# Expert stages of a six-stage block: VectorE makes both halves of the 0/1 routing matrix

## The chip, the cores and the metric

One core of one Trainium2 chip. The time is the device time of one execution of the whole kernel in microseconds. Five engines run their own instruction streams and meet at semaphores: PE (TensorE, with its weight loads shown apart as PEld), DVE (VectorE), ACT (ScalarE), POOL (GpSimd) and SP (SyncE, which here issues DMAs).

## The reference

The input x is 32 batches of 256 tokens with 128 channels. Six sub-layers follow one another: half a feed-forward layer, a gated attention unit, half a feed-forward layer, half an expert layer, linear attention, and half an expert layer again. Only the two expert layers bear on this case:

```
logits = x @ router_w + router_b                      # 8 experts
top_k_logits, expert_indices = top_k(logits, 2)
expert_probs = softmax(top_k_logits)
one_hot = one_hot(all first choices, then all second choices of a batch)
pos = cumsum(one_hot) * one_hot - 1                    # place of each token at its expert
expert_inputs[expert, pos] += x                        # 76 places for each expert and batch
o = (silu((in @ w_fc + b_fc) * (in @ w_gate + b_gate))) @ w_proj + b_proj
y = sum over the two choices of prob * o[expert, pos]
x = x + 0.5 * y
```

A place past the 76th is dropped. 8 experts of 76 places make 608 places ("slots") for each batch.

## The kernel before

A batch is two tiles (t = 0, 1) of 128 tokens, one token to a partition. An expert stage (`moe_stage`, run twice, as stages moe3 and moe5) groups the 32 batches into eight chunks of 2, 3, 5, 5, 5, 5, 5 and 2 batches. For one chunk, the eight experts are worked through one after another ("units"), each with four steps of the hidden dimension, so a chunk is 32 steps, here called work slots, numbered 0 to 31. In each work slot PE makes two products with 76 columns for each batch of the chunk (380 columns for five): `up`, L1538 and L1542. ACT adds a bias to the first (L1611), DVE multiplies both into `act` (L1715, `multiply`), ACT applies silu (L1618). At the end of each unit (every fourth work slot) PE makes the second layer of the unit before (`down`, L1552), DVE adds its bias (L1724) and SP stores the rows to memory.

Between these steps, the next chunk's batches are routed and the last chunk's results are brought back. The order is written out beforehand: each engine goes through the same list of work slots and does its own part of what is listed there. For the batch with index i of the next chunk the list says, counted from work slot 5i (9i in the first chunk and the one before the last): norm at +0, transpose at +1, router at +2, mask at +3, count at +4, assign at +5, hot0 at +8, hot1 at +9, send0 at +10, send1 at +11. In chunks with a step of 5, the hot0 of a batch and the mask of the next one share a work slot. Within a work slot DVE does first `multiply`, then norm, router, mask, assign, hot, `combine`, and then the bias of `down`; PE does first `up`, then router, transpose, count, send, and then `down`.

The parts that the change touches:

- `assign` (DVE) computes for each token the numbers of its two slots: `slot[..., 0:1]` for the first choice, `slot[..., 1:2]` for the second, and signals `routed` (L1697).
- `first_choice` (POOL, L1447) compares the row of slot numbers 1 to 608 with the first slot of each token and writes 0 or 1 in bf16 to `hot`, one instruction of 128x608 for each tile. POOL does it in its own order right after the `split` of the batch that has its norm in the same work slot, since it has nothing to do in hot0 and hot1: it is listed under assign (+5).
- `second_choice` (DVE, L1705) waits for `hot_first` (POOL's tile is there) and adds the comparison with the second slot to the same tile, at hot0 for tile 0 and at hot1 for tile 1.
- `send` (PE, L1526) waits for both tiles of `hot` and multiplies the tokens, split by POOL into three bf16 parts (`split`, L1436 to L1439), with `hot`: six matmuls for each half of the slots. ACT copies the result to `rowsT` (L1602), from which the next chunk's `up` reads.
- `hot` has two buffers. The one that writes first to a buffer waits for `sent_ps`, that the batch two before has been sent.
- `gather` (POOL, L1456): four indirect DMAs for each batch bring expert results back; `combine` (DVE, L1733) adds them to x. POOL gets to a gather five work slots ahead of its combine.

At the start of a stage, before the first work slot, the two batches of chunk 0 are routed with nothing beside them; `up` can't begin until both have been sent.

## Time and profile before

| | |
|---|---|
| Median of 3 runs | 2491.58 us (2489.34 to 2493.92) |
| Profiled execution, its own time | 2514.78 us |
| Its span, first to last instruction | 2512.8 us, 47937 instructions |
| Expert stages in that span | about 514 to 1070 us and 1916 to 2512 us |
| Mean granted TensorE clock | 0.967 of full speed |

The profiled execution took 23.2 us (0.9%) more than the median of the runs. All durations below are from the profiled execution. "Busy" is the time in which an engine had an instruction in work. A row of the timeline gives the start in us from the start of the span, the time in us, the engine, the source line, the operation, what it writes and what it reads, how many instructions were merged into the row, and in brackets the idle time of the engine just before and what ended it. "issue" there means that the profile shows nothing that the engine waited for.

### The profile page before, as it was taken

The numbers are of one execution on the slowest core, as the hardware profiler recorded it, in microseconds if no ns is written. First come the engines' busy times: TensorE is split into PE (matmuls) and PEld (weight loads), VectorE is DVE, ScalarE is ACT, GpSimd is POOL, SyncE is SP. The second block draws the span as 40 slices with busy tenths as digits, with TensorE's granted clock in tenths as the row PEclk, the third lists the DMA queues.
The fourth block names the chain that finished last, engine by engine and source line by source line (L and its number), as shares of the span: only waits on it lengthen the run. The fifth ranks groups of instructions, "written<-read, shape, count | busy, mean of one in ns | idle before, by whom it ended". The sixth has DMA issues, their size and how long they took to land.

```text
span 2512.8 us, 47937 instructions
## 1 busy us (share of the span) xinstructions
PE 2272.8 (90%) x14854; PEld 1816.3 (72%) x14854; DVE 1588.7 (63%) x4974; ACT 1312.6 (52%) x2713; POOL 733.7 (29%) x818
## 2 busy tenths in 40 slices
PE   3979998968999999849999999999996889999994
PEld 3979997957767676637777777777775776776773
DVE  5867776766667775435655656565655666767653
ACT  3755556744444444326666666666662544444441
POOL 2202220045546765320000000000002455766543
PEclk9989999989999999879999999999998999999997
DMA  7040000000111111100000000000000001111122
GB/s 242 0 159 0 0 0 0 0 5 23 26 28 40 41 36 41 46 18 1 0 0 0 0 0 0 0 0 0 0 0 0 15 25 35 43 50 45 49 56 50
DMA packets 70867, 67.45 MB, mean 27 GB/s; under 512 B 9696, under 2 KB 58336, under 8 KB 70368
## 3 DMA queue, kind: packets, MB, share of 16 engines
q1 hardware_dynamic: 61504, 47.16, 5.9%
q0 software_dynamic: 8192, 16.79, 2.9%
q10 hardware_dynamic: 1056, 2.10, 0.3%
q8 instruction: 56, 0.92, 0.2%
q14 instruction: 59, 0.48, 0.1%
HBM read 31.94 MB, written 34.08 MB: 26 GB/s over the span
## 4 chain that ended last, share of the span: by engine, by line
PE 48%; issue 4%; DVE 2%; POOL 1%; ACT 1%; DMA 0%; another core or an unknown queue 0%; ACTq 0%; POOLq 0%; DVEq 0%
PE moe_bank L1552 5%; PE lin_bank L983 5%; PE moe_bank L1538 5%; PE lin_bank L903 5%; PE moe_bank L1542 5%; PE lin_bank L911 4%; PE lin_bank L930 4%; PE lin_bank L922 4%; PE lin_bank L959 3%; PE lin_bank L975 2%; PE moe_bank L1526 2%; PE lin_bank L946 1%; POOL moe_landed L1456 1%; ACT lin_xT L1049 0%; PE moe_bank L1493 0%
## 5 line engine op out<-in xcount | busy, mean ns | idle before, releaser
L1611 ACT ACTIVATE moe_fc<-moe_bank,all_b_fc 128x380 f32<-128x380 f32 (+2 forms) x512 | 262.3, 513 | 341.7 <-PE moe_bank L1538 286.8
L1715 DVE SCALAR_TENSOR_TENSOR moe_act<-moe_bank,all_b_moe_gate,moe_fc 128x380 f32<-128x380 f32 (+2 forms) x512 | 271.0, 531 | 221.4 <-PE moe_bank L1542 106.9
L1538 PE MATMUL moe_bank<-moe_rowsT,all_w_fc 128*128 128x380 f32 (+2 forms) x1024 | 357.3, 431 | 15.6 <-ACT moe_fc L1611 12.8
L1542 PE MATMUL moe_bank<-moe_rowsT,all_w_gate 128*128 128x380 f32 (+2 forms) x1024 | 351.7, 425 | 12.9 <-DVE moe_act L1715 7.7
L1552 PEld LDWEIGHTS moe_bank<-all_w_proj,moe_act 128*128 128x128 f32 x2688 | 321.6, 195 | 12.4 <-ACT moe_act L1618 1.8
L1552 PE MATMUL moe_bank<-all_w_proj,moe_act 128*128 128x128 f32 x2688 | 329.2, 279 | 1.4 <-ACT moe_act L1618 1.4
L1456 POOL DMA_INDIRECT moe_landed<-rows_out,moe_take_at x256 | 266.0, 1039 | 176.2 <-issue 174.6
L1542 PEld LDWEIGHTS moe_bank<-moe_rowsT,all_w_gate 128*128 128x128 f32 x1024 | 188.3, 193 | 101.6 <-DVE moe_act L1715 8.9
L1447 POOL TENSOR_SCALAR moe_hot<-all_slot_ids,moe_slot 128x608 bf16<-128x608 f32 x128 | 233.3, 1830 | 91.7 <-issue 54.9
L1618 ACT ACTIVATE moe_act<-moe_act 128x760 f32<-128x760 f32 (+2 forms) x256 | 181.5, 709 | 96.0 <-DVE moe_act L1715 88.8
L1148 POOL COPY lin_xn_ones<-lin_xn 128x254 f32<-128x254 f32 x32 | 12.7, 398 | 748.0 <-PE lin_bank L911 743.3
L1053 ACT ACTIVATE lin_neg<-lin_bank 128x512 f32<-128x512 f32 x256 | 151.7, 592 | 95.3 <-PE lin_bank L903 50.7
L1538 PEld LDWEIGHTS moe_bank<-moe_rowsT,all_w_fc 128*128 128x128 f32 x1024 | 167.9, 193 | 43.6 <-ACT moe_fc L1611 13.5
L959 PEld LDWEIGHTS lin_bank<-lin_kv,lin_qT 128*128 128x128 f32 x1024 | 144.4, 191 | 63.4 <-issue 54.1
L1057 ACT ACTIVATE lin_neg<-lin_neg 128x512 f32<-128x512 f32 x256 | 161.1, 630 | 7.9
L1526 PE MATMUL moe_bank<-moe_hot,moe_parts 128*128 128x304 bf16 x768 | 125.5, 301 | 40.4 <-issue 24.7
L1081 ACT ACTIVATE lin_gate_tanh<-lin_bank,all_bg_half 128x256 f32<-128x256 f32 x256 | 103.5, 468 | 108.3 <-PE lin_bank L930 108.2
L1724 DVE TENSOR_TENSOR moe_expert_out<-moe_bank,all_b_proj 128x384 f32<-128x384 f32 (+1 forms) x128 | 64.8, 506 | 142.9 <-PE moe_bank L1552 108.4
L959 PE MATMUL lin_bank<-lin_kv,lin_qT 128*128 128x130 f32 x1024 | 151.9, 275 | 1.1 <-DVE lin_heads L1196 0.8
L1526 PEld LDWEIGHTS moe_bank<-moe_hot,moe_parts 128*128 128x128 bf16 x768 | 72.5, 100 | 96.3 <-issue 69.1
L903 PE MATMUL lin_bank<-all_wk,lin_xT 128*128 128x512 f32 x256 | 128.9, 607 | 4.5 <-ACT lin_xT L1049 2.7
L451 ACT ACTIVATE ffn_hT<-ffn_bank,all_b,all_alpha 128x256 f32<-128x256 f32 x256 | 123.6, 564 | 17.2 <-PE ffn_bank L407 17.2
(222 smaller groups left out, 4309.2 us busy)
## 6 DMA issues: line engine op xcount, KB each, us to landing
rows_out<-moe_expert_out SPq DMA_DIRECT2D x80, 128.0 KB
rows_out<-all_zeros SPq DMA_DIRECT2D x1, 9728.0 KB, 28.0
rows_out<-moe_expert_out SPq DMA_DIRECT2D x80, 62.0 KB
moe_landed<-rows_out,moe_take_at POOLq DMA_INDIRECT x256
out<-all_x SPq DMA_DIRECT2D x5, 640.0 KB
rows_out<-moe_expert_out SPq DMA_DIRECT2D x48, 64.0 KB
all_w_fc<-in_w_fc SPq DMA_DIRECT2D x1, 2048.0 KB, 9.8
all_w_gate<-in_w_gate SPq DMA_DIRECT2D x1, 2048.0 KB, 13.7
```

The costliest lines, as they stand in the source:

```text
L903: nc.tensor.matmul(bank[j][:, :], xT[:, j // 2 * P:(j // 2 + 1) * P], k.wk[:, j % 2 * HU:(j % 2 + 1) * HU], start=True, stop=True).then_in ...
L959: last = nc.tensor.matmul(bank[4 + n % 2][:, i * 2 * DH1:(i + 1) * 2 * DH1], qT[:, p, t * P:(t + 1) * P], kv[:, p, :], start=True, stop=True)
L1057: nc.scalar.activation(neg[:, j, :], neg[:, j, :], ACT.Exp, scale=-1.0).then_inc(exps.sem, 1)
L1447: nc.gpsimd.tensor_scalar(hot[:, b % 2, t, :], k.slot_ids[:, :], slot[:, b % 2, t, 0:1], None, ALU.is_equal).then_inc(hot_first, 1)
L1456: nc.gpsimd.indirect_dma_start(landed[:, b % LANDED, t, h, :], None, k.rows_out, bass.IndirectOffsetOnAxis(take_at[:, i, h:h + 1], 0), bou ...
L1526: last = nc.tensor.matmul(bank[SENT][:, 0:HALF], parts[:, b % PARTS, q, t, :], hot[:, b % 2, t, h * HALF:(h + 1) * HALF], start=(t == 0 an ...
L1538: nc.tensor.matmul(bank[FC + j % 2][:, 0:c.width], k.w_fc[:, e, j * P:(j + 1) * P], rowsT[:, c.n % 2, e, 0:c.width], start=True, stop=True ...
L1542: nc.tensor.matmul(bank[GATE + j % 2][:, 0:c.width], k.w_gate[:, e, j * P:(j + 1) * P], rowsT[:, c.n % 2, e, 0:c.width], start=True, stop= ...
L1552: last = nc.tensor.matmul(bank[OUT][:, j * DIM:(j + 1) * DIM], act_in[:, i % 2, h, j * P:(j + 1) * P], k.w_proj[:, e * MC + h, :], start=( ...
L1611: nc.scalar.activation(fc[:, j, 0:c.width], bank[FC + j % 2][:, 0:c.width], ACT.Identity, bias=k.b_fc[:, e * MC + j:e * MC + j + 1]).then_ ...
L1618: nc.scalar.activation(a, a, ACT.Silu).then_inc(act_sb, 1)
L1715: nc.vector.scalar_tensor_tensor(act_in[:, i % 2, j, 0:c.width], bank[GATE + j % 2][:, 0:c.width], k.b_moe_gate[:, e * MC + j:e * MC + j + ...
```

## The change

VectorE makes both comparisons. `first_choice` and its semaphore are gone from POOL's program. In DVE's hot0 and hot1, and in its start of the stage, `second_choice` becomes `choices`: it compares with the first slot, waits for that result, and then adds the comparison with the second one. The wait for the buffer of the batch two before moves from POOL to DVE. `choose_masks` no longer waits for POOL's comparisons of the batch two before. `assign`, `send` and all work slots stay as they are.

```
             @block.gpsimd
-                def first_choice(b):
-                    pool.wait_ge(routed, b + 1)
-                    if b >= 2:
-                        pool.wait_ge(sent_ps, 2 * (b - 2) + 2)
-                    for t in range(TILES):
-                        nc.gpsimd.tensor_scalar(hot[:, b % 2, t, :], k.slot_ids[:, :], slot[:, b % 2, t, 0:1], None,
-                                                ALU.is_equal).then_inc(hot_first, 1)
...
-                for b in plan[0].batches:
-                    first_choice(b)
...
-                        if "assign" in work:
-                            first_choice(work["assign"])
...
             @block.vector
                     if b >= 2:
-                        dve.wait_ge(hot_first, TILES * (b - 1))
                         dve.wait_ge(count_ps, b - 1)
...
-                def second_choice(b, t):
-                    dve.wait_ge(hot_first, TILES * b + t + 1)
+                def choices(b, t):
                     dve.wait_ge(routed, b + 1)
+                    if b >= 2:
+                        dve.wait_ge(sent_ps, 2 * (b - 2) + 2)
+                    link(nc.vector.tensor_scalar(hot[:, b % 2, t, :], k.slot_ids[:, :], slot[:, b % 2, t, 0:1], None, ALU.is_equal))
                     nc.vector.scalar_tensor_tensor(hot[:, b % 2, t, :], k.slot_ids[:, :], slot[:, b % 2, t, 1:2], hot[:, b % 2, t, :],
                                                    ALU.is_equal, ALU.add).then_inc(hot_sb, 1)
...
                     for t in range(TILES):
-                        second_choice(b, t)
+                        choices(b, t)
...
                             if f"hot{t}" in work:
-                                second_choice(work[f"hot{t}"], t)
+                                choices(work[f"hot{t}"], t)
```

`link` gives the instruction a semaphore and lets DVE wait for it before its next instruction.

## Rows read from the trace of the kernel before

**Rows 1.** The page, part 1: busy time of each engine and share of the span.

```profile
PE 2272.8 (90%) x14854; PEld 1816.3 (72%) x14854; DVE 1588.7 (63%) x4974; ACT 1312.6 (52%) x2713; POOL 733.7 (29%) x818
```

**Rows 2.** Windows, one chunk: PE, PEld, DVE, ACT, POOL busy; clock; DMA share; GB/s.

```profile
740.00:817.00 77.00, 75.64 (x446) 54.40 (x445) 55.55 (x185) 36.41 (x68) 50.57 (x50) 1.00 0.15 39
```

**Rows 3.** Groups of instructions: busy us, mean ns | idle before, releasers.

```profile
L1447 POOL TENSOR_SCALAR moe_hot<-all_slot_ids,moe_slot 128x608 bf16<-128x608 f32 x128 | 233.3, 1830 | 91.7 <-issue 54.9 <-DVE moe_slot L1697 32.8
...
L1526 PE MATMUL moe_bank<-moe_hot,moe_parts 128*128 128x304 bf16 x768 | 125.5, 301 | 40.4 <-issue 24.7 <-DVE moe_hot L1705 12.0 <-ACT moe_rowsT L1602 3.2
...
L1705 DVE SCALAR_TENSOR_TENSOR moe_hot<-all_slot_ids,moe_slot,moe_hot 128x608 bf16<-128x608 f32 x128 | 112.9, 882 | 4.6 <-POOL moe_hot L1447 3.9 <-issue 0.2
...
L1436 POOL CAST moe_parts<-moe_xn 128x256 bf16<-128x256 f32 x64 | 28.1, 439 | 247.8 <-DVE moe_xn L261 176.2 <-issue 71.2
```

**Rows 4.** Timeline of the second expert stage: a send (chunk of five, first batch).

```profile
2152.62 0.61 DVE L1715 SCALAR_TENSOR_TENSOR moe_act<-moe_bank,all_b_moe_gate,moe_fc 128x380 f32<-128x380 f32 x1 [0.82 <-PE moe_bank L1542]
...
2153.60 0.85 DVE L1705 SCALAR_TENSOR_TENSOR moe_hot<-all_slot_ids,moe_slot,moe_hot 128x608 bf16<-128x608 f32 x1
...
2154.36 0.61 DVE L1715 SCALAR_TENSOR_TENSOR moe_act<-moe_bank,all_b_moe_gate,moe_fc 128x380 f32<-128x380 f32 x1
2154.58 0.80 PE L1542 MATMUL moe_bank<-moe_rowsT,all_w_gate 128*128 128x380 f32 x2
...
2154.88 0.84 DVE L1705 SCALAR_TENSOR_TENSOR moe_hot<-all_slot_ids,moe_slot,moe_hot 128x608 bf16<-128x608 f32 x1
...
2155.80 0.64 PEld L1526 LDWEIGHTS moe_bank<-moe_hot,moe_parts 128*128 128x128 bf16 x6 [1.03 <-issue]
2155.83 0.93 PE L1526 MATMUL moe_bank<-moe_hot,moe_parts 128*128 128x304 bf16 x6 [0.45 <-issue]
```

**Rows 5.** Timeline: the same of the chunk's third batch.

```profile
2179.29 0.84 DVE L1705 SCALAR_TENSOR_TENSOR moe_hot<-all_slot_ids,moe_slot,moe_hot 128x608 bf16<-128x608 f32 x1
...
2181.98 0.10 PEld L1526 LDWEIGHTS moe_bank<-moe_hot,moe_parts 128*128 128x128 bf16 x1
```

**Rows 6.** Timeline: the same of the chunk's fourth batch.

```profile
2192.60 0.61 DVE L1715 SCALAR_TENSOR_TENSOR moe_act<-moe_bank,all_b_moe_gate,moe_fc 128x380 f32<-128x380 f32 x1 [0.82 <-PE moe_bank L1542]
```

**Rows 7.** Groups of DVE instructions, shapes kept apart.

```profile
L261 DVE TENSOR_SCALAR ffn_xn<-all_x,ffn_mean,ffn_rstd 128x128 f32 x128 | 38.7, 345 | 13.8 <-issue 11.8
...
L773 DVE TENSOR_SCALAR gau_lin_qT<-gau_qkT,all_os_gamma,all_os_beta 128x256 f32<-128x256 f32 x33 | 13.6, 411 | 0.0
...
L384 DVE CAST all_tri<-all_tri_in 128x128 bf16<-128x128 f32 x1 | 0.2, 228 | 0.0
```

**Rows 8.** Timeline: two instructions of `assign` joined by `link`.

```profile
2157.12 0.17 DVE L1694 TENSOR_SCALAR moe_over<-moe_pos 128x4 f32<-128x4 f32 x1
2157.32 0.36 DVE L1695 SCALAR_TENSOR_TENSOR moe_over<-moe_top_atf,moe_over 128x4 f32<-128x4 f32 x1
```

**Rows 9.** Timeline: DVE beside POOL's comparisons, splits and gathers.

```profile
702.61 3.60 POOL L1447 TENSOR_SCALAR moe_hot<-all_slot_ids,moe_slot 128x608 bf16<-128x608 f32 x2
...
705.56 0.68 DVE L1679 CAST moe_top_atf<-moe_top_at 128x4 f32<-128x4 uint32 x1
...
2155.62 1.00 POOL L1456 DMA_INDIRECT moe_landed<-rows_out,moe_take_at  x1 [0.30 <-issue]
...
2156.16 0.60 DVE L261 TENSOR_SCALAR moe_xn<-all_x,moe_mean,moe_rstd 128x128 f32<-128x128 f32 x2
```

**Rows 10.** Timeline: start of the first expert stage.

```profile
529.06 0.68 DVE L1699 TENSOR_SCALAR moe_prob<-moe_tanh_gap 128x2 f32<-128x2 f32 x1
...
531.54 1.35 DVE L1705 SCALAR_TENSOR_TENSOR moe_hot<-all_slot_ids,moe_slot,moe_hot 128x608 bf16<-128x608 f32 x1 [0.43 <-POOL moe_hot L1447]
...
533.04 1.68 PE L1526 MATMUL moe_bank<-moe_hot,moe_parts 128*128 128x304 bf16 x6 [6.01 <-DVE moe_hot L1705]
```

**Rows 11.** Timeline: second batch routed beside the chunk of three (228 columns).

```profile
609.92 0.15 DVE L1684 SCALAR_TENSOR_TENSOR moe_row_base<-moe_top_atf,all_batch_row 128x4 f32<-128x4 f32 x1
610.78 1.35 DVE L1705 SCALAR_TENSOR_TENSOR moe_hot<-all_slot_ids,moe_slot,moe_hot 128x608 bf16<-128x608 f32 x1 [0.70 <-POOL moe_hot L1447]
```

More of the change, by code:

```diff
@@ L1341, in moe_stage @@
         routed = k.sem("routed")
-        hot_first = k.sem("first_choice_hot")
         hot_sb = k.sem("hot_ready")
```

## The prediction

> **What bounds the kernel now.** I began with the page's busy times: PE has 90% of the span [rows 1]. An average over six stages doesn't decide, so the next view was the windows, one for each chunk of an expert stage. In a chunk of five batches PE is busy 75.64 of 77 us at full clock, DVE 55.55, POOL 50.57 [rows 2]. There, whatever holds PE lengthens the kernel, and little else does. The third view was the groups: PE's send (L1526) has 40.4 us of idle time before it, 24.7 of it "issue", and 12.0 put down to DVE's hot. DVE waits for POOL's comparisons only 3.9 us in all [rows 3].
>
> "issue" names no culprit, so the last view was the timeline around each of the 64 sends. There the second comparison of tile 1 starts at 2154.88 and takes 0.84 [rows 4], so it ends at about 2155.73 (to the ns of the trace). The send's first weight load starts at 2155.80, 0.07 us later, and PE had been idle 0.45 us. I read the same pair for all batches: in 50 of 64 the weights come 0.07 us after the end of hot1. The send waits for hot in nearly every batch; the profile just doesn't say so. The DVE chain in front is pinned to PE at its head: the multiply of hot0's work slot begins after 0.82 us of idle time, upon PE's product [rows 4]. From there DVE works without a gap (multiply, masks, hot0, multiply, hot1) until hot1 is done, and PE can't start the send. Anything put into this chain goes into the time of PE, and PE has no idle time elsewhere in the chunk to take it back: 77 less 75.64 us, most of it these very waits.
>
> **What the change removes.** POOL loses 128 comparisons of 1.83 us, 233.3 us of busy time [rows 3]. POOL is no bound in the chunks [rows 2]: they are done before DVE needs them, but for 8 waits of 3.9 us together, and they start right behind the split. Worth nothing by themselves. They hinder DVE, though: see below.
>
> **What it adds.** 128 comparisons on DVE, one operand in SBUF in f32, one pointer scalar, 608 elements, bf16 out. The trace has no such instruction, so I size it from relatives [rows 7]. The same kind with two pointer scalars takes 345 ns for 128 elements and 411 for 256: 66 ns for 128 elements, 0.515 ns each. To 608 elements that is 345 + 480 x 0.515 = 592 ns with two pointers. A cast to bf16 without pointers takes 228 ns for 128 elements, so each pointer costs about 58 ns, and one pointer gives 592 - 58 = 0.53 us. Bounds: without any pointer's cost 0.475, with both 0.59; and if a comparison ran at the pace of L1705, 0.844 [rows 4], a far upper bound, since L1705 reads two tensors. I take 0.53, from the rows of the same kind. `link` then makes the second comparison wait: an instruction of 0.17 from 2157.12 is followed by its reader at 2157.32, 0.03 us after its end [rows 8]. Each tile adds d = 0.53 + 0.035 = 0.565 us. The added waits (routed, the send of two batches before) are long fulfilled: the send in question is at work slot 5i+1, hot0 at 5i+8.
>
> What queues behind it: on DVE the multiply of the next work slot. PE needs that one only for the product two work slots on, after the send, so it holds nothing before the send does. Behind the send wait all later products of PE, in order. They move by the same amount as DVE's chain, both from the end of hot1, so no second stall is to be expected.
>
> **The sum, batch by batch**, over the 60 batches that are routed inside work slots:
> - 8 batches have their hot1 early: 2179.29 + 0.84 = 2180.13 against a send at 2181.98 [rows 5]. PE is in `down` and has 1.85 us (1.57 in one) of other work. Two tiles cost 1.13: nothing.
> - 7 batches are like [rows 6]: between hot0 and hot1 DVE waits 0.82 us for PE's product behind a `down`. The tile of hot0 disappears in that; one counts: 7d.
> - 2 batches have 0.735 us to spare (2d - 0.735 each), 1 has 0.43 (2d - 0.43), 2 have 0.14 (2d - 0.14 each).
> - 2 batches are like [rows 11], where hot0 waited for POOL. The comparison could begin at 610.00, hot1 would be done at 610.00 + 2d + 1.98 instead of 612.56 + 0.85 = 613.41: 2d - 1.43 each.
> - The other 40 pay both tiles: 80d.
>
> Together 97d - 5.0 = 54.8 - 5.0 = 49.8 us.
>
> **The start of each stage.** The first send came at 533.04 after 6 us of waiting for hot, DVE waited for POOL's tiles 0.43 at a time, and its comparison took 1.35 instead of 0.84 beside POOL's [rows 10]. Now DVE is free for the first tile at about 529.2 (the 0.68 of L1699 is such a hindrance too), and two tiles of 1.41, overlapped by 0.08, end at 531.94 instead of 532.89. Gain 0.9 for each stage, 1.8 in all; the second batch's send is held by PE and ACT.
>
> **DVE beside POOL.** A DVE cast of four elements took 0.68 us instead of 0.16 until POOL's comparison ended (702.61 + 3.60 = 706.21) [rows 9]. It lies in the chain of one of the 40 batches, once in each stage: 1.0 us gained. The other such delays (combine has most of them) end in DVE idle time before the next multiply. Against it, in the stretches with a step of nine, norm stands just before hot1; POOL's split (0.44 for its first piece, L1436 [rows 3]) gets between first and second comparison in 6 batches, 0.4 each: 2.4 us lost.
>
> Sum: 49.8 - 1.8 - 1.0 + 2.4 = +49.4 us. The profiled execution should go from 2514.8 to about 2564, the median, 23 us lower and on the same program, from 2491.6 to 2541.0 (+2.0%).
>
> **The gathers.** Before, a gather started after POOL's comparisons and ran beside hot0 and hot1; now it starts about 3.6 us earlier, right after the split, and combine's data land earlier. Combine isn't in the chain, so no gain. Whether a gather holds up the new comparison must be asked: in rows 9 two instructions of that kind took 0.60 for both, their usual pace, in the midst of a gather's instruction; of 43 such meetings the median is 342 ns, as without one. So I add nothing.
>
> The Trainium skill, page "SBUF — State Buffer", section "Who interferes with whom", says that a VectorE instruction in a mode with two ports and any GpSimd instruction shut each other out for the whole instruction. The cast that waited for POOL's comparison agrees; the two instructions beside the gather don't, if the gather's instruction counts. Applied to gathers too, the rule makes the second rival below.
>
> **Rivals.**
> 1. *The comparison runs at the pace of L1705*: 0.844 us, d = 0.88. Then 97 x 0.88 - 5.0 = 80.4, the start gains only 0.3 for each stage: 80.4 - 0.6 - 1.0 + 2.4 = +81, 2573 us. Against it speaks the slope of 0.515 ns in rows 7, for it that no comparison stands among these rows. Chance 0.08.
> 2. *Gathers hold up the comparison.* A gather's instruction takes 1.00 [rows 9]; half of it on average for each of the 97 tiles in the chain would be +49 more: 2590 us. The 43 meetings speak against it. Chance 0.04.
> 3. *Part is given back.* If ACT or the second send had a wait that the delay now fills, half might return: +25, 2516 us. For it: PE idles in other places as well, around `count`. Against it: 1.4 us in 77 is all there is [rows 2]. Chance 0.10.
> 4. *The other side: no slower.* The 0.07 us could be what the send's own start costs, with PE held by its queue ("issue" in rows 4), and not by hot1. Then the 0.45 us before the send cover part of 1.13, the spare time the rest, and only the start's 1.8 and the 1.0 are left: 2489 us, which is within what this kernel's measurement can tell from no change (0.2%, 5 us). It would take over from the forecast if fewer than 5 / 0.565 = 9 tiles lay in the chain. Against it: 50 equal distances of 0.07 with idle times of PE between 0.04 and 2.2. Chance 0.06, of which 0.02 for a gain over 0.2%.
> 5. *Something beyond, such as DVE becoming the bound.* 55.55 + 10 x 0.53 = 61 of then 81 us in a chunk: no [rows 2]. Chance 0.02, slower.
>
> **How the numbers follow.** The forecast has 0.70 and from the bounds of d (0.51 to 0.625, so 97d - 5.0 from 44 to 56) its own range of 2535 to 2548. Cases 1 and 3 enclose it at 2573 and 2516; with them the range 2516 to 2574 leaves out about 0.12 and the edges of those two. Slower by over 0.2%: 0.70 + 0.08 + 0.04 + 0.10 + 0.02 = 0.94; within 0.2% 0.04; faster 0.02.
>
> **What would show it.** The new comparison 128x608 at about 0.53 us, the one behind it 0.03 later at 0.84. The send's weights still 0.07 after hot1 and PE idle about 1.6 before it where rows 4 have 0.45; the third batch of each chunk unchanged. A chunk of five takes 77 + 7 x 0.565 = 81 us, with 75.6 of PE busy as before. POOL's busy time falls by 233 us, to 500. The prediction is wrong if the comparison is far from 0.53, if the chunk doesn't grow by 4 us, or if the idle time before the send grows but shrinks elsewhere.

## The result and the profile after

| | before | after |
|---|---|---|
| Median | 2492.75 us (2489.34 to 2494.98, 4 runs) | 2544.11 us (2541.59 to 2544.87, 4 runs) |
| Ratio | | 1.0206, 95% interval 1.0194 to 1.0219 |
| Profiled execution, its own time | 2514.78 us | 2544.87 us |

The change costs 51.4 us; the prediction said 49.4 (2541.0, range 2516 to 2574). The two profiled executions are only 30 us apart, and the profiled one of after is 19 us below the 2564 that the prediction gave for it: the one of before lost some 22 us, over both expert stages, in waits put down to "remote" behind the last send of a stage, and the one of after has none of these. The sections below therefore compare distances between sends, which lie ahead of those waits. Of all executions reported here one, of experiment 3, is far off the others (7893 us against 2489 to 2499), and nothing on record explains it.

The page's first part and one chunk as a window (the counterparts of [rows 1] and [rows 2]; the window is now 81 us wide, columns as there):

```profile
PE 2275.4 (89%) x14854; PEld 1817.8 (71%) x14854; DVE 1638.8 (64%) x5102; ACT 1313.8 (52%) x2713; POOL 500.8 (20%) x690
```

```profile
740.00:821.00 81.00, 75.58 (x446) 54.28 (x445) 59.38 (x196) 36.61 (x68) 31.87 (x40) 1.00 0.14 35
```

POOL has lost 232.9 us of busy time and 128 instructions. The same chunk, with the same 446 matmuls and the same busy time of PE at full clock, takes 81 us instead of 77. PE does no more; it waits more.

The groups of the comparisons with their shapes kept apart, and then the page's group of the send (the counterparts of [rows 3]):

```profile
L1692 DVE TENSOR_SCALAR moe_hot<-all_slot_ids,moe_slot 128x608 bf16<-128x608 f32 x128 | 68.1, 532 | 0.1
L1693 DVE SCALAR_TENSOR_TENSOR moe_hot<-all_slot_ids,moe_slot,moe_hot 128x608 bf16<-128x608 f32 x128 | 109.0, 852 | 4.6
```

```profile
L1513 PE MATMUL moe_bank<-moe_hot,moe_parts 128*128 128x304 bf16 x768 | 129.3, 308 | 84.2 <-issue 71.0
```

The new comparison takes 532 ns on average (forecast 0.53). The idle time ahead of the send has doubled, 40.4 to 84.2 us, and nearly all of the increase has no culprit in the profile: "issue" went from 24.7 to 71.0. The timeline names it. This is the send of [rows 4], 26 us later by now:

```profile
2177.37 0.61 DVE L1703 SCALAR_TENSOR_TENSOR moe_act<-moe_bank,all_b_moe_gate,moe_fc 128x380 f32<-128x380 f32 x1 [0.82 <-PE moe_bank L1529]
...
2178.30 0.99 POOL L1447 DMA_INDIRECT moe_landed<-rows_out,moe_take_at  x1 [0.30 <-issue]
2178.42 0.53 DVE L1692 TENSOR_SCALAR moe_hot<-all_slot_ids,moe_slot 128x608 bf16<-128x608 f32 x1
2178.98 0.85 DVE L1693 SCALAR_TENSOR_TENSOR moe_hot<-all_slot_ids,moe_slot,moe_hot 128x608 bf16<-128x608 f32 x1
2179.74 0.61 DVE L1703 SCALAR_TENSOR_TENSOR moe_act<-moe_bank,all_b_moe_gate,moe_fc 128x380 f32<-128x380 f32 x1
2180.27 0.53 DVE L1692 TENSOR_SCALAR moe_hot<-all_slot_ids,moe_slot 128x608 bf16<-128x608 f32 x1
2180.83 0.85 DVE L1693 SCALAR_TENSOR_TENSOR moe_hot<-all_slot_ids,moe_slot,moe_hot 128x608 bf16<-128x608 f32 x1
2181.75 0.64 PEld L1513 LDWEIGHTS moe_bank<-moe_hot,moe_parts 128*128 128x128 bf16 x6 [2.23 <-issue]
2181.78 0.94 PE L1513 MATMUL moe_bank<-moe_hot,moe_parts 128*128 128x304 bf16 x6 [1.66 <-issue]
```

The chain still begins with 0.82 us of waiting for PE and has no gap. The last comparison ends at 2181.68, the send's weights come 0.07 us later, and PE's idle time went from 0.45 to 1.66 us. The third batch of the chunk (the counterpart of [rows 5]) still has time to spare:

```profile
2207.51 0.85 DVE L1693 SCALAR_TENSOR_TENSOR moe_hot<-all_slot_ids,moe_slot,moe_hot 128x608 bf16<-128x608 f32 x1
...
2209.07 0.10 PEld L1513 LDWEIGHTS moe_bank<-moe_hot,moe_parts 128*128 128x128 bf16 x1
```

Its comparison ends at 2208.36, 0.71 us ahead of the send, where 1.85 us were spare before: the difference is 1.14, two tiles. I took the distance from each send to the next in both traces (start of the first weight load):

| stretch | before, us | after, us | difference |
|---|---|---|---|
| to a full batch (for example the 17th) | 12.20 | 13.34 | +1.14 |
| to a third batch | 13.98 | 13.98 | 0.00 |
| to a fourth batch | 12.06 | 12.63 | +0.57 |
| to the batch with index 13, either stage | 12.48 | 13.10 | +0.62 |
| 40 steady distances (ends at index 10 to 29, both stages) | 617.6 | 651.4 | +33.8 |
| 18 distances in the chunks of 2 and 3 (ends at index 1 to 9) | 227.1 | 239.8 | +12.7 |
| last two of each stage | 95.3 | 100.3 | +5.0 |
| all 62 | 940.0 | 991.4 | +51.4 |

The start of the first stage, up to its first send (the counterpart of [rows 10]):

```profile
528.42 0.54 DVE L1692 TENSOR_SCALAR moe_hot<-all_slot_ids,moe_slot 128x608 bf16<-128x608 f32 x1
...
530.33 0.85 DVE L1693 SCALAR_TENSOR_TENSOR moe_hot<-all_slot_ids,moe_slot,moe_hot 128x608 bf16<-128x608 f32 x1
...
531.33 1.68 PE L1513 MATMUL moe_bank<-moe_hot,moe_parts 128*128 128x304 bf16 x6 [5.02 <-DVE moe_hot L1693]
```

The send comes 1.71 us earlier, but the stage itself began 0.73 us earlier in this execution, as POOL's first instruction of the stage shows (before, after):

```profile
514.40 2.66 POOL L1465 MEMSET moe_act<- 128x3072 f32 x1 [123.77 <-POOLq L319]
```

```profile
513.67 2.66 POOL L1456 MEMSET moe_act<- 128x3072 f32 x1 [123.77 <-POOLq L319]
```

Counted from there, the first send is 0.99 us earlier in the first stage and 0.97 in the second.

**One thing that the prediction had no term for** is the clock. The windows from 541 to 590 us, before and after:

```profile
541.00:590.00 49.00, 42.28 (x334) 38.05 (x333) 29.36 (x117) 25.23 (x67) 20.27 (x22) 1.00 0.04 12
```

```profile
541.00:590.00 49.00, 40.78 (x307) 36.95 (x307) 28.66 (x110) 22.05 (x59) 6.63 (x11) 0.93 0.04 11
```

PE gets through 307 matmuls instead of 334, and the mean granted clock is 0.93 instead of 1.00. The timeline shows a stretch; first the 16 weight loads of a `down` after, then the same `down` before:

```profile
568.27 1.00 PE L1513 MATMUL moe_bank<-moe_hot,moe_parts 128*128 128x304 bf16 x6 [0.95 <-issue]
...
568.91 3.48 PEld L1539 LDWEIGHTS moe_bank<-all_w_proj,moe_act 128*128 128x128 f32 x16
```

```profile
568.01 1.88 PEld L1552 LDWEIGHTS moe_bank<-all_w_proj,moe_act 128*128 128x128 f32 x16
```

3.48 instead of 1.88 us: the clock is at the lower level, 1.2 GHz. Ahead of it PE had been idle for 0.95 us before the send and for 1.54 shortly before that. From the first product of each stage to 30 us before its last, the clock stands at the lower level for 6.8 us before (two places) and 30.7 us after (nine). What one such place costs can be read from the trace of after, since both stages run the same program: the distance to the batch with index 7 is 12.34 us in the first stage, with 3.4 us at the lower level in it, and 10.64 in the second, with none; the one to index 10 is 26.86 with none and 28.53 with 3.4 us. So a place costs about 1.7 us, half of its length, and the seven more places about 12 us. Of these seven, four lie in the chunks of 2 and 3, one in a steady distance, and one right behind the last send of each stage.

### The profile page after: what moved, and what is told of

Its sections match the earlier page's. It is cut to its first block, busy times and chain, and to the rows that moved or that the text cites. A ratio compares the mean times of both kernels' runs of the same rounds, so it can differ in the third digit from the quotient of the medians.

```text
span 2542.8 us, 47839 instructions
## 1 busy us (share of the span) xinstructions
PE 2275.4 (89%) x14854; PEld 1817.8 (71%) x14854; DVE 1638.8 (64%) x5102; ACT 1313.8 (52%) x2713; POOL 500.8 (20%) x690
## 4 chain that ended last, share of the span: by engine, by line
PE 46%; issue 5%; DVE 2%; ACT 1%; POOL 1%; DMA 0%; ACTq 0%; POOLq 0%; DVEq 0%
PE moe_bank L1539 5%; PE lin_bank L983 5%; PE lin_bank L903 5%; PE lin_bank L911 4%; PE lin_bank L930 4%; PE moe_bank L1525 4%; PE lin_bank L922 4%; PE moe_bank L1529 4%; PE lin_bank L959 3%; PE lin_bank L975 2%; PE moe_bank L1513 2%; PE lin_bank L946 1%; POOL moe_landed L1447 1%; ACT lin_xT L1049 0%; PE moe_bank L1480 0%
## 5 line engine op out<-in xcount | busy, mean ns | idle before, releaser
L1529 PE MATMUL moe_bank<-moe_rowsT,all_w_gate 128*128 128x380 f32 (+2 forms) x1024 | 351.5, 425 | 10.9 <-DVE moe_act L1703 10.9
L1539 PEld LDWEIGHTS moe_bank<-all_w_proj,moe_act 128*128 128x128 f32 x2688 | 323.4, 196 | 12.5 <-ACT moe_act L1605 1.6
L1529 PEld LDWEIGHTS moe_bank<-moe_rowsT,all_w_gate 128*128 128x128 f32 x1024 | 188.1, 192 | 99.7 <-DVE moe_act L1703 14.1
L1513 PE MATMUL moe_bank<-moe_hot,moe_parts 128*128 128x304 bf16 x768 | 129.3, 308 | 84.2 <-issue 71.0
L1513 PEld LDWEIGHTS moe_bank<-moe_hot,moe_parts 128*128 128x128 bf16 x768 | 73.5, 102 | 142.1 <-issue 113.9
L1589 ACT COPY moe_rowsT<-moe_bank 128x304 f32<-128x304 f32 x128 | 52.8, 413 | 185.9 <-PE moe_bank L1513 185.9
L1435 POOL CAST moe_parts<-moe_xn 128x256 bf16<-128x256 f32 x64 | 26.7, 418 | 565.5 <-DVE moe_xn L261 360.7
```

Source lines behind the costliest of these rows:

```text
L1513: last = nc.tensor.matmul(bank[SENT][:, 0:HALF], parts[:, b % PARTS, q, t, :], hot[:, b % 2, t, h * HALF:(h + 1) * HALF], start=(t == 0 an ...
L1529: nc.tensor.matmul(bank[GATE + j % 2][:, 0:c.width], k.w_gate[:, e, j * P:(j + 1) * P], rowsT[:, c.n % 2, e, 0:c.width], start=True, stop= ...
L1539: last = nc.tensor.matmul(bank[OUT][:, j * DIM:(j + 1) * DIM], act_in[:, i % 2, h, j * P:(j + 1) * P], k.w_proj[:, e * MC + h, :], start=( ...
```

## The experiments

Nine kernels in twelve runs, three groups of four, each group on one chip with the kernel before beside it: 2494.72 us in the first group, 2520.13 in the second, 2515.64 in the third (13 executions each). On the first chip no trace has waits put down to "remote" in the expert stages; on the other two all have (experiment 7), so a time of the first group can't be compared with one of the others, only distances without such a wait can.

**1. The first comparison twice** (first group), the changed kernel with

```
-                    link(nc.vector.tensor_scalar(hot[...], k.slot_ids[:, :], slot[..., 0:1], None, ALU.is_equal))
+                    for _ in range(2):
+                        link(nc.vector.tensor_scalar(hot[...], k.slot_ids[:, :], slot[..., 0:1], None, ALU.is_equal))
```

> The comparison with the first slot is made twice for each tile (the output stays the same). Theory 1 (everything put between the multiply of hot0's work slot and the end of hot1 goes into PE's time): a second d of 0.57 us for each of the 97 tiles that lie in the chain, 55 us, and since the spare time of the 8 'third' batches (0.70 us left in the changed kernel) and of the 7 'fourth' ones (0.25 left) is now exceeded, 8 x 0.43 + 7 x 0.32 = 5.7 more: +61 over the changed kernel, 2605 us, the weights of the send still 0.07 us after hot1. Rival (the slowdown of the change is not DVE's chain but something that came once, such as another layout of the instruction streams or PE's clock): less than +20, below 2565.

Measured: 2639.62 us, ratio 1.0575 (1.0556 to 1.0594), +95 us over the changed kernel. In the undisturbed steady batches the second comparison costs what the first did or less: 12.26 to 13.40 us, 13.34 to 14.49, the fourth 12.63 to 12.92, and now the third too, 13.98 to 14.49, since its spare time is used up. For the rest, the time at the lower clock rose from 31 to 99 us, now in the steady chunks as well. There 12 of the 40 distances hold 3.1 to 5.8 us of it; these are 1.5 to 2.8 us longer than the same distance without it (15.97 instead of 14.49, 16.12 instead of 14.49), 20 us together, and no other distance is. At half of its length, as in the trace of after, (99 - 31) / 2 = 34 us is the gap between +95 and the +61 of the theory. The waits of PE, of this kernel:

```profile
PE moe_bank L1513 <- issue: 126.0, 52, 3.6
```

So the work in the chain is paid in full, and the lower clock comes on top. That PE's longer idling brings it is the candidate that experiment 5 asks about.

**2. DVE makes the first comparison of tile 0 only**, POOL that of tile 1 (first group), the kernel before with

```
-                    for t in range(TILES):
+                    for t in range(1, TILES):
                         nc.gpsimd.tensor_scalar(hot[:, b % 2, t, :], ...).then_inc(hot_first, 1)
...
+                    if t:
+                        dve.wait_ge(hot_first, b + 1)
+                    else:
+                        link(nc.vector.tensor_scalar(hot[:, b % 2, t, :], ..., ALU.is_equal))
```

> The kernel before, but VectorE makes the first comparison of tile 0 (at hot0) and GpSimd that of tile 1. Theory 1: tile 0's comparison counts in the 40 full batches and in 3 others, not in the fourth batches of the chunks of five, where DVE waits 0.82 us for PE between hot0 and hot1: 43 x 0.565 - 0.7 = +24, 2516 us. Rival (what costs is that DVE has any such instruction beside gathers, or the sum of its work): the same per tile everywhere, 60 of 120 tiles, half of the measured +51, with the fourth batches paying as well.

Measured: 2512.32 us, ratio 1.0070 (1.0054 to 1.0087). The full batches grow by 0.58 (12.20 to 12.78), the fourth ones not at all (12.06 both), the third ones neither. In the steady chunks that is the prediction's count tile by tile: tile 0's comparison disappears in DVE's wait of 0.82 us between hot0 and hot1 in the fourth batches, and is paid in the full ones. The sum was missed, +17.6 us instead of +24: the chunks of 2 and 3 grew by 0.7 us, where the count has 13 tiles less 0.7, 6.6 us. The lower clock doesn't explain it: it took 19.7 us of these 18 distances, and 21.5 in the kernel before.

**3. The first comparisons where DVE has time** (first group): both still on DVE, but at work slots +5 and +6 of the batch, the second ones left at +8 and +9.

```
-"hot0": 8, "hot1": 9,
+"first0": 5, "first1": 6, "hot0": 8, "hot1": 9,
...
+                            if f"first{t}" in work:
+                                first(work[f"first{t}"], t)
                             if f"hot{t}" in work:
-                                choices(work[f"hot{t}"], t)
+                                second(work[f"hot{t}"], t)
```

> The changed kernel with the same 128 comparisons on VectorE, but moved ahead in its list: tile 0 at +5 behind assign, tile 1 at +6; the second comparisons stay at hot0 and hot1. Theory 1: DVE has idle time there before hot0's work slot, so the chain from multiply to hot1 is as long as before the change, and the whole +51 is gone: 2490 us, 3 below before through the start of the stages and the missing hindrance by GpSimd. Rival 1 (VectorE has too much work, wherever it stands): 2544 as in the changed kernel. Rival 2 (half of the idle time is too short for it): about 2505.

Measured: 2494.22 us, ratio 0.9996 (0.9986 to 1.0006). The same 128 comparisons on the same engine cost nothing, although they are slower there, 622 ns on average instead of 532; the distances between sends are those of the kernel before. PE's wait is back as well:

```profile
PE moe_bank L1513 <- issue: 22.9, 48, 1.2
```

This is the strongest run for the theory: not the work of DVE costs, but its place behind a product of PE and in front of a send. VectorE having too much to do (rival 1) is out. It was run on the first group's chip alone.

**4. Both comparisons of both tiles earlier**, at +6 and +7 (first group).

```
-"hot0": 8, "hot1": 9,
+"hot0": 6, "hot1": 7,
```

> The changed kernel with hot0 at +6 and hot1 at +7 in place of +8 and +9, send unchanged at +10 and +11. Theory 1: the send finds hot ready, its weights come right behind the product before, and PE's idle time before the sends, 24 us over both stages in the kernel before, is gone as well: 2466 us, faster than both. Rival 1 (the 0.07 us is the send's own start, the idle time stays): 2490 at best. Rival 2 (hot0 beside combine makes the multiplies late, and PE waits for these instead): 2490 to 2540, with PE's idle time before the products of L1529.

Measured: 2515.41 us, ratio 1.0074 (1.0054 to 1.0094). The theory's 2466 is missed by 49 us, and the time lies in the range of rival 2. The wait before the send is gone ("issue" no longer stands among the waits of L1513), but another has come, and not at the products of L1529, where the rival had it:

```profile
PE moe_bank L1497 <- DVE moe_mask L1666: 51.1, 45, 2.5
```

PE's `count` stands one work slot after DVE's mask; at +7 of a batch the next batch has its router, at +8 its mask, and the hot instructions in front make the mask late. The send's wait was moved to `count`. A step of this list is free only if nothing behind it in DVE's order feeds PE soon.

**5. Two comparisons, with PE kept at work** (second group, and again in the third): the kernel of 1, with six more matmuls into the send's bank before PE waits for hot; their result is overwritten. The wait for that bank (`sent_sb`) had to move ahead of the one for hot with them, and the third batches of the chunks of five have no such matmuls.

```
+                    if b or h:
+                        pe.wait_ge(sent_sb, 2 * b + h)
...
+                        for q in range(6):
+                            nc.tensor.matmul(bank[SENT][:, 0:HALF], parts[...], parts[...], start=True, stop=True)
                         pe.wait_ge(hot_sb, TILES * (b + 1))
-                    if b or h:
-                        pe.wait_ge(sent_sb, 2 * b + h)
```

> As the kernel with the comparison made twice (2640 us, 34 more than the waits alone should give), but PE fills part of each long wait before a send with six matmuls of 304 columns whose result is overwritten (0.94 us at full clock; left out in the third batches of the chunks of five, where there is no such wait). Theory 1a (the 34 us are half-clock stretches that follow PE's waits: 96 us at 0.5 in that kernel between the sends, 31 in the changed kernel, 7 before): with shorter idle times the half-clock stretches shrink to under 30 us, the sends stay where DVE puts them, and the time falls by about 30 us to 2608. Rival (DVE's chain itself got longer than it was reckoned, PE's clock only follows): no less than 2635, more if the fillers delay the sends.

> First comparison made twice, and six more matmuls before the send's wait, so that PE works while DVE compares. Theory of the clock: the one with two comparisons alone took 2639.6, of which about 32 us came from stretches at half clock; with PE at work in the wait they go, and the time is about 2608 (ratio 1.046). Rival: the stretches don't come from PE's wait before the send, or the added matmuls cost what the clock gives back: 2635 or more (ratio 1.056 or more).

Measured: 2675.74 us, ratio 1.0619 (1.0602 to 1.0637), and in the third group 2663.70, 1.0585 (1.0568 to 1.0603). Both totals are on the rival's side, and the 40 steady distances barely fell: 704.5 and 703.2 us against 705.2 in experiment 1. Distance by distance the traces say something else. At the lower clock stand 17 us of the steady distances in each, instead of 44, in 5 of the 40 distances instead of 12. Where it doesn't stand, the distances are those of experiment 1 (14.46, 13.37, 14.52 us against 14.49, 13.41, 14.49), and only the fourth batches come 0.1 to 0.7 us later, so the extra matmuls cost little there. What took the gain away is the fifth batches of the chunks of five: six of them come after 14.4 to 15.0 us instead of 13.4, at full clock, and each of these six distances has an ACT or a DVE that waits for "remote", as here in the third group:

```profile
825.93 0.58 ACT L1603 ACTIVATE moe_fc<-moe_bank,all_b_fc 128x380 f32<-128x380 f32 x1 [3.03 <-remote]
```

Experiment 1 was run on the chip without such waits, so the totals can't be compared. PE at work in the wait does keep the clock up in most places, as the theory has it; what it would gain on one chip wasn't measured.

With the edit, the profile also names the culprit that it had called "issue" (waits of PE, third group; below it the waits of the kernel before):

```profile
PE moe_bank L1518 <- DVE moe_hot L1699: 94.0, 48, 6.2
```

```profile
PE moe_bank L1526 <- issue: 24.7, 42, 2.2
PE moe_bank L1526 <- DVE moe_hot L1705: 12.0, 2, 6.0
```

This need not be the matmuls. In the kernel before, PE waits for hot first and for the bank last, right in front of the send; the only two sends that the profile puts down to hot are the first of each stage, the ones for which the program has no wait for the bank. In experiment 5 hot comes last, and is named. Which of the two does it was not tried apart.

**6. POOL goes on comparing for nobody** (second and third group): the changed kernel, with POOL's comparisons of the kernel before, into a tile that nothing reads.

```
+        spare = k.sb("spare_hot", [P, 2, TILES, EXPERTS * CAP], BF16)
...
+                        nc.gpsimd.tensor_scalar(spare[:, b % 2, t, :], k.slot_ids[:, :], slot[:, b % 2, t, 0:1], ...)
```

> The changed kernel, but GpSimd still makes its 128 comparisons where it made them before, into a tile that nobody reads. It tells what GpSimd's absence is worth. Theory 1: 1 us for each stage's start, 0.5 for each of the two blocked casts, and the combines' delays end in idle time: +2 to +6 over the changed kernel, 2546 to 2550. Rival (GpSimd's comparisons were a real hindrance to DVE, and the change gains by their absence what it loses less elsewhere): +15 or more.

> POOL still makes its comparisons, into a tile that nobody reads, while DVE makes both. Theory: POOL's freed time is worth next to nothing, so +0 to +8 us over the changed kernel of this group (ratio to it 1.000 to 1.003). Rival: DVE beside POOL's comparisons loses much more than I counted (the second group's 1.0286 against 1.0206, +20 us), so +15 to +25 over the changed kernel again.

Measured: 2592.15 us, 1.0286 (1.0268 to 1.0303), and 2588.89 us, 1.0293 (1.0276 to 1.0310). The first, by its ratio, looked like +20 us over the changed kernel; but the changed kernel itself had been timed on another chip only. Beside it (experiment 7, 2589.97 us) the difference is -1 us, and this total is a sum of parts that cancel. The window of the same chunk, in the third group:

```profile
740.00:821.00 81.00, 75.64 (x445) 54.30 (x444) 58.48 (x190) 36.28 (x69) 49.16 (x49) 1.00 0.13 34
```

POOL is busy 49.16 us there instead of 31.87, and the chunk takes the same 81 us (the 40 steady distances: 653.4, experiment 7 has 654.2, the first trace of after 651.4). 233 us of POOL's time are worth next to nothing there. In the chunks of 2 and 3 they cost 12 us, 253.4 against 241.4, where DVE's new comparison takes 681 ns on average instead of 533 and the clock is lower for longer (48.7 instead of 36.0 us), and in the starts of the stages 1.6 us each (the first send 19.23 instead of 17.62 us after the stage's start). The loss was made up by the last distance of each stage, 20.5 us shorter together than in experiment 7; why, experiment 7 shows. So with both comparisons on DVE, POOL's silence is worth some 15 us outside the steady chunks, more than the theory's 0 to 8, and the -1 is luck.

**7. The changed kernel again** (third group), no edit.

> The changed kernel once more, as the measure for the other three of this group. In the second group of runs the kernel before took 2520 us where the first group had 2495, and its rows had stalls put down to 'remote'. If what I have shown of the change holds on any chip, the ratio to the kernel before is 1.0206 again, within 0.002 (2546 us where the kernel before takes 2495). If the stalls and the clock of a chip take part in the loss, the ratio comes out above 1.023 on a chip where the kernel before takes 2520.

Measured: 2589.97 us, ratio 1.0292 (1.0275 to 1.0309). The steady distances are those of the first trace to 0.01 us, but for one of 29.09 instead of 29.15 and for fourth batches (up to +0.74). The rest of the difference lies at few places, above all in the last distance of each stage: 32.10 and 32.26 us instead of 21.85 and 21.87. The timeline there shows engines that start long after what they need:

```profile
1020.23 0.61 DVE L1703 SCALAR_TENSOR_TENSOR moe_act<-moe_bank,all_b_moe_gate,moe_fc 128x380 f32<-128x380 f32 x1 [1.29 <-remote]
1020.47 0.80 PE L1525 MATMUL moe_bank<-moe_rowsT,all_w_fc 128*128 128x380 f32 x2
...
1024.43 0.58 ACT L1598 ACTIVATE moe_fc<-moe_bank,all_b_fc 128x380 f32<-128x380 f32 x1 [5.03 <-remote]
...
1028.57 0.92 PE L1525 MATMUL moe_bank<-moe_rowsT,all_w_fc 128*128 128x380 f32 x2 [1.90 <-issue]
...
1030.16 0.61 DVE L1703 SCALAR_TENSOR_TENSOR moe_act<-moe_bank,all_b_moe_gate,moe_fc 128x380 f32<-128x380 f32 x1 [3.28 <-remote]
```

The product that ACT takes up at 1024.43 was done at 1021.27. Such waits come to 95 us over ACT and DVE together in this trace (many at the same time on both):

```profile
ACT moe_fc L1598 <- remote: 47.9, 16, 6.9
DVE moe_expert_out L1712 <- remote: 26.2, 7, 7.4
DVE moe_act L1703 <- remote: 21.1, 9, 5.3
```

The profiled execution of before has them only behind the last send of each stage: from there to the end of the stage it takes 22 us more, both stages together, than experiment 3 on the first chip. The first trace of after has them nowhere in the expert stages. The two traces with the waits can be compared directly: from before to experiment 7 the distances grow by 76.5 us, the starts give 1.9 back, and the stretches behind the last sends are alike to 1.3 us, 76 us together against 74.3 between the medians. So on such a chip the change costs 74 us, on the other 51.

What the stalls are is open, but the rows show where they are. In the changed kernel POOL, free of its comparisons, issues the sixteen gathers of four batches one after another ahead of the last send, each 1.30 us after the last (here the first and the last of experiment 7):

```profile
1011.55 1.03 POOL L1447 DMA_INDIRECT moe_landed<-rows_out,moe_take_at  x1 [0.77 <-POOL moe_parts L1438]
...
1031.11 1.00 POOL L1447 DMA_INDIRECT moe_landed<-rows_out,moe_take_at  x1 [0.30 <-issue]
```

In the kernels in which POOL still compares, the same gathers come as four and twelve, with the comparisons between them (experiment 6, third group):

```profile
1022.70 1.00 POOL L1457 DMA_INDIRECT moe_landed<-rows_out,moe_take_at  x1 [0.30 <-issue]
1028.20 3.61 POOL L1448 TENSOR_SCALAR moe_spare_hot<-all_slot_ids,moe_slot 128x608 bf16<-128x608 f32 x2 [4.50 <-DVE moe_slot L1698]
1031.98 1.10 POOL L1457 DMA_INDIRECT moe_landed<-rows_out,moe_take_at  x1 [0.17 <-issue]
```

On the chips of the second and third group the last distance is stalled in all four traces with sixteen in a row (31.9 to 35.8 us in experiments 5, 7 and 9) and in none with four and twelve (19.5 to 22.3 in experiments 6 and 8). All kernels issue sixteen in a row once more behind the last send, and there all have the stalls on these chips. On the first chip sixteen in a row stall nothing. It isn't code that loads: the trace of experiment 7 has no packet of an instruction queue between 1013.5 and 1050 us. Why some chips stall and others don't, no run tells.

**8. The second comparison cut by halves of the slots** (second and third group): the kernel before; hot0 works the first 304 slots of both tiles, hot1 the others, and each half of the send waits for its own.

```
-                        pe.wait_ge(hot_sb, TILES * (b + 1))
+                    pe.wait_ge(hot_sb, 2 * TILES * b + TILES * (h + 1))
...
+                    for t in range(TILES):
+                        at = slice(h * HALF, (h + 1) * HALF)
+                        nc.vector.scalar_tensor_tensor(hot[:, b % 2, t, at], ...).then_inc(hot_sb, 1)
```

> The kernel before, GpSimd's comparisons included, but the second comparison is cut by slots and not by tiles: at hot0 VectorE finishes slots 1 to 304 of both tiles, at hot1 slots 305 to 608, and the send of a half waits for its own half alone. It costs DVE four instructions of about 0.53 in place of two of 0.84 for each batch (+0.4). Theory 1 (PE waits before the send for hot1, and for nothing else): the first send's half is ready one work slot earlier, PE's idle time before the sends (24 us) goes, and the time falls to about 2470. Rival (the 0.07 us is the send's own start, or the multiplies get late by the 0.4): 2490 to 2500.

> The kernel before, with the second comparisons cut by halves of the slots, again. Theory: the shorter intervals between sends seen in the second group (0.5 us in most batches) are real, and the longer first chunk was that chip's clock: then -15 to -25 us, 2470 to 2480 where the kernel before takes 2495, ratio 0.990 to 0.994. Rival: the first chunk is longer with this kernel whatever the chip, and the total stays at 1.000 (2490 to 2500).

Measured: 2522.04 us, 1.0006 (0.9997 to 1.0016), and 2514.07 us, 0.9987 (0.9977 to 0.9996). Two instructions of 304 take 1.0 us where one of 608 took 0.85, but the send no longer waits: PE's "issue" before it is down from 24.7 to 5.9 us.

```profile
PE moe_bank L1526 <- issue: 5.9, 4, 2.4
```

In the steady chunks that is worth what it should be: full batches 12.20 to 11.84, 12.06 to 11.54, 11.11 to 10.61, the 40 distances 617.6 to 603.4, -14.2 us. The third batches got 0.38 longer, and the chunks of 2 and 3 gave back 9.0 (227.1 to 236.1; 241.2 in the second group), and the theory's gain of 15 to 25 us did not come. So the longer first chunks are mostly the kernel's own, as the rival had it, and in both groups the time differs from no change by less than 0.2%, by -0.13% where the interval leaves out 1.

**9. The kernels of 3 and 8 together** (second group).

> VectorE makes both comparisons, the first ones at +5 and +6, the second ones cut by slots as in the run beside it. Theory 1: the same as that run and 3 us less, since GpSimd no longer delays the start of each stage: 2467 us. Rival (DVE now has so much to do in every work slot that its multiplies hold PE): above 2480, with PE's idle time before L1529 in place of that before the sends.

Measured: 2551.26 us, ratio 1.0120 (1.0104 to 1.0137). Missed by 84 us. The undisturbed steady distances are those of experiment 8 or within 0.25 us, but the trace has stalls like those of experiment 7: six of the eight fifth batches take 14.4 to 17.1 us instead of 10.6, the last distance of a stage 31.9 instead of 19.5, and 68 us stand at the lower clock. It was run on one chip only. What the kernel takes on a chip without stalls is open.

## Why the prediction was right, point by point

- **The bound** (PE in the chunks, nothing else). Right: 75.58 of 81 us after, 75.64 of 77 before, and 49.16 or 31.87 us of POOL make no difference there (experiment 6).
- **The send waits for hot1, and the profile calls it "issue".** Right: 0.07 us again, experiments 1, 2 and 3 lengthen and shorten the wait with the chain in front of it, and experiment 5 makes the profile say it.
- **The comparison costs 0.53 and `link` 0.035.** Right: 0.532, and 0.57 for a tile against 0.565. Rival 1 (0.844) is out.
- **97 tiles less 5.0 us, 49.8.** The classes are right in the steady chunks: +1.14, +0.57 and 0.00 for full, fourth and third batches, and experiment 2 shows them apart. The list has a slip: the classes named before "the other 40" hold 22 of the 60 batches, so 38 are left, 76d, and only with 76 do the tiles come to the 97 that the sum uses. In the chunks of 2 and 3 the count is too high: 31 tiles less 5.0 us are 12.5 us, and 12.7 were measured, but of these some 7 are the four more places at the lower clock. Experiment 2 has the same gap without the clock (0.7 us instead of 6.6). The misfit is largest at the batch with index 8, where the distance fell from 11.53 to 10.86 and the count has it grow; why is open.
- **The start, -1.8.** Right: -2.0 (0.99 and 0.97). DVE's first comparison starts at 528.42, which is 529.15 in the times of before, for 529.2 forecast.
- **The blocked cast, -1.0.** Right: the cast at 705.56 [rows 9] is in the chain of the batch with index 13, and its distance grows by 0.62 instead of 1.14 in both stages: 1.04 gained. With POOL comparing again (experiment 6) it is 0.14 to 0.54 longer.
- **POOL's split between the comparisons, +2.4.** Wrong: beside the split the second comparison takes 0.862 to 0.866 us instead of 0.851, and it is POOL that waits, where the first piece of the split took 0.58 and the next 1.09 us:

```profile
566.95 0.58 POOL L1435 CAST moe_parts<-moe_xn 128x256 bf16<-128x256 f32 x1 [12.80 <-issue]
...
567.60 1.09 POOL L1436 TENSOR_TENSOR moe_rest<-moe_xn,moe_parts 128x256 f32<-128x256 f32 x1
```

- **The gathers, nothing.** Right: the gather now runs beside the comparison (2178.30 in the timeline above), and in 30 such meetings the median is 526 ns, in the other 98 it is 528. Rival 2 is out. The rule of the Trainium skill that stood behind it, page "SBUF — State Buffer", section "Who interferes with whom", is borne out in these rows for POOL's instructions that compute (the new comparison took 587 instead of 532 ns in experiment 6), and not for the one that issues a gather.
- **Rivals 3, 4 and 5** (part given back; no slower; DVE the bound): the distances grow by whole tiles, a second comparison adds rather than hides, and DVE is busy 59.38 of 81 us.

The sum, part by part. "Lower clock" is an estimate, 1.7 us for each place more than before, from the rows of the trace of after.

| part | forecast, us | measured, us | of it lower clock, us |
|---|---|---|---|
| 40 steady distances | 58 tiles, 32.8, less the cast's 1.0: 31.8 | 33.8 | 1.7 |
| 18 distances in the chunks of 2 and 3 | 31 tiles less 5.0, 12.5, and the split's 2.4: 14.9 | 12.7 | 6.8 |
| last two distances of each stage | 8 tiles: 4.5 | 5.0 | 0 |
| starts | -1.8 | -2.0 | 0 |
| behind the last sends (against experiment 3) | 0 | 3.4 | 3.4 |
| sum | 49.4 | 52.9, medians 51.4 | 12 |

So the mechanism is right, and 36 of the 49 us (steady and last distances) are right to within 0.5 us once the clock's 1.7 are set apart. The rest is partly luck: in the chunks of 2 and 3 a count that is some 6 us too high and a +2.4 that did not come were made up by a lower clock that the prediction did not have. That the clock falls because PE idles longer before the sends fits experiments 1 and 5, and the price of a place at the lower level is read from equal distances; which wait brings which place was not traced. For the 74 us on the chips with stalls (experiment 7) the prediction has no term: it had POOL's freed time as worth nothing.

## What to carry to other kernels

Work that moves to an engine "with time to spare" is paid in full if it lands between a wait for the bounding engine and that engine's next need, and costs nothing a few steps earlier (+51 us and 0 for the same 128 instructions, the change and experiment 3). Look for a fixed small distance between an instruction's end and the start of the one that idles, since the profile may call such a wait "issue", here where another wait stood between it and the send. Time taken off an idle engine isn't free either: what that engine does next moves forward and bunches (the sixteen gathers). Compare kernels on the same chip: the same pair had a ratio of 1.0206 on one and 1.0292 on another, and one experiment was misread by 20 us for want of a run of the changed kernel beside it.

## What the runs showed of the hardware

- **The granted clock fell where PE's waits grew.** With waits before the send that are 0.6 to 1.1 us longer, the window from 541 to 590 us went from a clock of 1.00 to 0.93 (rows above). With matmuls put into the waits of the kernel with two comparisons, 17 instead of 44 us of the steady distances stood at the lower level. A place of 3.4 us at the lower level made its distance 1.5 to 1.8 us longer. With the comparison made twice the window stands at 0.87:

```profile
541.00:590.00 49.00, 37.58 (x264) 33.00 (x265) 27.68 (x108) 20.42 (x54) 7.85 (x12) 0.87 0.03 9
```

- **DVE and POOL hold each other up in both directions**, but not for the same price: DVE's comparison 534 to 587 ns, on average over the kernel, with POOL's comparisons going on (experiments 7 and 6 on one chip), and POOL's subtraction 0.67 to 1.09 us beside DVE's.
- **A gather's instruction of 1.00 us on POOL holds up nothing** on DVE (526 against 528 ns).
- **Stalls of up to 7.4 us on ACT and DVE** (experiment 7), with PE behind them, which the profile puts down to "remote", recur at the same place in both stages on some chips, above all where POOL issues sixteen gathers in a row, and are missing in the same program on another. The kernel before took 2493 and 2495 us in two of the groups of runs and 2516 and 2520 in the two others, the changed one 2544 and 2590.
